# Broadcast row maxima put into query order by GpSimd once per group, with a new job order

## The reference, cut to what matters

```python
xn = layernorm(x)                      # x: 1 x 2048 x 256, eps 1e-5, no affine part
k, q, v = (einsum('ihd,bpd->biph', W, xn) for W in (W_K, W_Q, W_V))      # 16 heads of 128
scores = einsum('biph,biqh->biqp', k, q)
masked = scores * tril - 1e10 * (1 - tril)
attn = softmax(masked / sqrt(128), axis=-1)
s = einsum('df,bqf->bqd', W_O, concat_heads(attn @ v))
base = xn @ W_base.T + b_base
onehot = one_hot(argmax(softmax(xn @ router_W.T)), 8)                    # one of 8 experts of rank 16
g = silu(base + 2.0 * ((xn @ A) * onehot) @ Bw)
return x + s * g
```

## Time and profile before

| | |
|---|---|
| median of three runs | 1547.8 us |
| profiled execution, its own time | 1548.1 us |
| its span, first to last instruction | 1546.2 us |
| mean granted TensorE clock | 0.989 of full speed |
| score tiles, seeds of them by ScalarE | 640 |
| groups (head, g), each with its two DMAs | 64 |

### The profile page before, as it was taken

The page is one execution under the profiler, slowest core; times in us unless marked ns, Lnnn a source line. Parts: engine busy times, 40 slices in busy tenths (PEclk is TensorE's granted clock), DMA queues, the critical chain, the costliest instruction groups (busy, mean ns, idle before and its releaser), DMA issues.

```text
span 1546.2 us, 23204 instructions
## 1 busy us (share of the span) xinstructions
PE 1459.5 (94%) x7788; PEld 1193.2 (77%) x7788; DVE 1248.1 (81%) x2541; ACT 1274.0 (82%) x2196; POOL 793.4 (51%) x688
## 2 busy tenths in 40 slices
PE   5999999999999999999999999999999999999997
PEld 4877778777877878777787777877787777877765
DVE  6788877888788886888868887788878898788864
ACT  2788898889888898898988888888987988888962
POOL 2444655455465555456554555554645555544740
PEclk9899999999999999999999999999999999999998
DMA  2100010000100001000010001000010000100002
GB/s 75 49 8 14 15 25 25 15 15 8 29 21 15 15 7 42 15 14 13 10 42 15 7 15 28 22 15 14 8 35 21 15 7 13 40 8 15 15 28 82
DMA packets 30070, 33.75 MB, mean 22 GB/s; under 512 B 11008, under 2 KB 17664, under 8 KB 29952
## 3 DMA queue, kind: packets, MB, share of 16 engines
q1 hardware_dynamic: 29952, 32.26, 8.3%
HBM read 30.02 MB, written 2.23 MB: 21 GB/s over the span
## 4 chain that ended last, share of the span: by engine, by line
PE 51%; ACT 24%; DVE 13%; issue 9%; POOL 2%; DMA 0%; SPq 0%; ACTq 0%; POOLq 0%; DVEq 0%
PE ps L281 15%; PE ps L282 14%; PE ps L283 14%; ACT ps L478 7%; ACT probs L498 7%; ACT p_hi L499 6%; DVE p_lo L551 6%; PE ps L719 4%; DVE partmax L566 3%; POOL colsum L433 2%; PE ps L754 2%; ACT qT_hi L486 1%; DVE z_lo L588 1%; ACT z_hi L504 1%; PE ps L731 1%
## 5 line engine op out<-in xcount | busy, mean ns | idle before, releaser
L433 POOL TENSOR_TENSOR colsum<-colsum,probs 128x512 f32<-128x512 f32 (+3 forms) x512 | 610.2, 1192 | 388.3 <-ACT probs L498 373.6
L478 ACT ACTIVATE ps<-maxrow 128x512 f32<-128x512 f32 (+3 forms) x640 | 645.3, 1008 | 8.9 <-DMA maxrow<-max_dram 8.7
L551 DVE TENSOR_TENSOR p_lo<-probs,p_hi 128x512 fp32r<-128x512 f32 (+3 forms) x640 | 614.9, 968 | 42.4 <-ACT p_hi L499 41.4
L498 ACT ACTIVATE probs<-ps 128x512 f32<-128x512 f32 (+3 forms) x640 | 362.9, 567 | 141.4 <-PE ps L731 74.8
L499 ACT ACTIVATE p_hi<-ps 128x512 fp32r<-128x512 f32 (+3 forms) x640 | 365.3, 571 | 0.0
L566 DVE TENSOR_REDUCE partmax<-ps 128x1 f32<-128x512 f32 x384 | 256.9, 679 | 10.4 <-PE ps L719 9.5
L281 PE MATMUL ps<-qT_hi,kT_hi 128*128 128x512 f32 (+3 forms) x640 | 247.6, 387 | 12.7 <-ACT ps L478 9.6
L281 PE MATMUL ps<-p_hi,v_hi 128*128 128x512 f32 (+3 forms) x640 | 241.7, 378 | 13.2 <-DVE p_lo L551 12.2
L282 PE MATMUL ps<-qT_lo,kT_hi 128*128 128x512 f32 (+3 forms) x640 | 234.3, 366 | 0.0
L283 PE MATMUL ps<-qT_hi,kT_lo 128*128 128x512 f32 (+3 forms) x640 | 233.9, 366 | 0.0
L282 PE MATMUL ps<-p_lo,v_hi 128*128 128x512 f32 (+3 forms) x640 | 233.5, 365 | 0.0
(11 more groups left out here) (106 smaller groups left out, 2174.8 us busy)
## 6 DMA issues: line engine op xcount, KB each, us to landing
maxrow<-max_dram SPq DMA_DIRECT2D x64, 256.0 KB, 3.8
wraw<-wqk_dram SPq DMA_DIRECT2D x16, 256.0 KB, 3.8
acc<-x_dram SPq DMA_DIRECT2D x4, 512.0 KB, 7.2
wraw<-wv_dram SPq DMA_DIRECT2D x8, 256.0 KB, 4.7
wraw<-wo_dram SPq DMA_DIRECT2D x8, 256.0 KB, 2.9
probs<-x_dram SPq DMA_DIRECT2D x4, 512.0 KB, 4.5
out_dram<-acc SPq DMA_DIRECT2D x4, 512.0 KB, 3.0
max_dram<-rowmax SPq DMA_DIRECT2D x64, 2.0 KB, 1.4
```

What stands on the lines that cost most here:

```text
L433: nc.gpsimd.tensor_tensor(total[:, c0:], total[:, c0:], tile[:, c0:], ALU.add)\
L478: nc.scalar.activation(st[job.n % SCORE_BANKS].rearrange("p (t n) -> p t n", t=TB)[:, q:, :], maxrow[:, job.g, :].rearrange("p (n t) -> p ...
L498: nc.scalar.activation(probs[:, k, c0:], src, ACT.Exp, scale=SCALE).then_inc(probs_ready, 1)
L551: nc.vector.tensor_tensor(p_lo[:, k, c0:], probs[:, k, c0:], f32(p_hi[:, k, c0:]), ALU.subtract)\
```

## The change

GpSimd gets a new step, `order_maxima`: for each group it copies the broadcast row from a new buffer `spread` (two slots, used in turn) into `maxrow`, reading with a step of four elements and writing with step one, so that `maxrow` is in query order. ScalarE's seed reads `maxrow` with step one, waits at a group's first tile for GpSimd's `max_ordered` in place of the DMA, and writes the same columns as before. The step stands in GpSimd's queue ahead of the sum of tile min(slot of the last maximum + 6, first tile of the group - 2), and the first two groups' ahead of tile 0. It waits for the DMA and, from the second head on, for the seeds of the same g of the head before. SyncE's broadcast DMA waits for the copy two blocks back (`max_ordered`) in place of those seeds.

`SCHEDULE` holds the same 216 jobs in another order. The slots of the last maximum of each group (in the pair's 80 slots; first tile of the next pair's groups counted on from 80):

| group (head of the pair, g) | first score tile | last maximum before | after | copy ahead of tile |
|---|---|---|---|---|
| (0, 2) | 12 | 5 | 5 | 10 |
| (0, 3) | 24 | 18 | 17 | 22 |
| (1, 0) | 40 | 28 | 33 | 38 |
| (1, 1) | 44 | 37 | 37 | 42 |
| (1, 2) | 52 | 46 | 43 | 49 |
| (1, 3) | 64 | 58 | 57 | 62 |
| next (0, 0) | 80 | 73 | 71 | 77 |
| next (0, 1) | 84 | 79 | 79 | 82 |

The diff, with most of the written-out order cut:

```diff
--- before.py
+++ after.py
@@ -33,6 +33,7 @@
 PROBS = LAG + 1
 SCORE_BANKS = 3
 SEED_AHEAD = 2
+ORDER_LAG = 6
 AUX_BANKS = 3
 MASKED = -1.0e10
 SCALING = 2.0
@@ -101,16 +102,16 @@
 
 
 SCHEDULE = (
-    "V00 w Pq03 V01 w w z7 | | Pk02 | s7 Pk03 v V11 | o70 v M0222 | M0212 o71 v M0202 M0232 v | V21 S0 Z0 | v V10 "
...
 )
 AFTER_LAST = "w w w z7 s7 o70 o71"
 
@@ -186,6 +187,7 @@
         colsum = sb("colsum", [P, 2, BW])
         partmax = sb("partmax", [P, NB, TB, NB])
         rowmax = sb("rowmax", [P, NB, TB])
+        spread = sb("spread", [P, 2, BW])
         maxrow = sb("maxrow", [P, NB, BW])
         rinv = sb("rinv", [P, 2, TB])
         acc = sb("acc", [P, NT, D])
@@ -239,7 +241,8 @@
         aux_free = sem("aux_free")
         max_ready = sem("max_ready")
         max_out = sem("max_out")
-        max_spread = [sem(f"max_spread{g}") for g in range(NB)]
+        max_spread = [sem(f"max_spread{k}") for k in range(2)]
+        max_ordered = sem("max_ordered")
         bits_set = sem("bits_set")
         seeded = sem("seeded")
         scores_ready = sem("scores_ready")
@@ -267,6 +270,15 @@
             return NB + b if head % 2 and b < 2 else b
 
         scores = [job for job in plan if isinstance(job, Score)]
+        first_tile = {job.head * NB + job.g: job.n for job in scores if job.kt == 0}
+        max_blocks = [job.head * NB + job.g for job in plan if isinstance(job, RowMax) and job.last]
+
+        order_at, tile = [], 0
+        for job in plan:
+            if isinstance(job, Score):
+                tile = job.n + 1
+            elif isinstance(job, RowMax) and job.last:
+                order_at.append(tile and min(tile - 1 + ORDER_LAG, first_tile[job.head * NB + job.g] - SEED_AHEAD))
 
         def columns(t):
 
@@ -340,9 +352,10 @@
                     sp.wait_ge(max_ready, blocks)
                     sp.dma_start(row.rearrange("(p t) -> p t", t=TB), rowmax[:, job.g, :]).then_inc(max_out, 16)
                     sp.wait_ge(max_out, 16 * blocks)
-                    if job.head:
-                        sp.wait_ge(seeded, tiles_until((job.head - 1) * NB + job.g))
-                    sp.dma_start(maxrow[:, job.g, :], row.partition_broadcast(P)).then_inc(max_spread[job.g], 16)
+                    k = (blocks - 1) % 2
+                    if blocks > 2:
+                        sp.wait_ge(max_ordered, blocks - 2)
+                    sp.dma_start(spread[:, k, :], row.partition_broadcast(P)).then_inc(max_spread[k], 16)
                 if not isinstance(job, Score):
                     continue
                 i, at, last = job.n // TILES, job.n % TILES, job.n // TILES == PAIRS - 1
@@ -410,14 +423,27 @@
             split_weights(wraw[:, 0, :], flat(wqk_hi[:, 0]), flat(wqk_lo[:, 0]), wqk_in, 16, 1, wqk_ready)
             split_weights(wraw[:, 1, :], flat(wv_hi[:, :, :]), flat(wv_lo[:, :, :]), wv_in, 16, 2, wv_ready)
 
+            def order_maxima(block):
+
+                gi = max_blocks[block]
+                pool.wait_ge(max_spread[block % 2], 16 * (block // 2 + 1))
+                if gi >= NB:
+                    pool.wait_ge(seeded, tiles_until(gi - NB))
+                nc.gpsimd.tensor_copy(maxrow[:, gi % NB, :].rearrange("p (t n) -> p t n", t=TB),
+                                      spread[:, block % 2, :].rearrange("p (n t) -> p t n", t=TB))\
+                  .then_inc(max_ordered, 1)
+
             normed_jobs = sum(isinstance(job, Normed) for job in plan)
             pool.wait_ge(aux_full, normed_jobs)
             nc.gpsimd.memset(acc[:, :, :], 0.0).then_inc(acc_clear, 1)
-            his = 2
+            his, ordered = 2, 0
             for job in plan:
                 if not isinstance(job, Score):
                     continue
                 n, c0 = job.n, columns(job)
+                while ordered < len(max_blocks) and order_at[ordered] <= n:
+                    order_maxima(ordered)
+                    ordered += 1
                 gi = job.head * NB + job.g
                 total, tile = colsum[:, gi % 2, :], probs[:, n % PROBS, :]
                 pool.wait_ge(probs_ready, n + 1)
@@ -473,11 +499,10 @@
                 if job.n >= SCORE_BANKS:
                     act.wait_ge(hi_ready, job.n - SCORE_BANKS + 1)
                 if job.kt == 0:
-                    act.wait_ge(max_spread[job.g], 16 * (job.head + 1))
-                q = columns(job) // P
-                nc.scalar.activation(st[job.n % SCORE_BANKS].rearrange("p (t n) -> p t n", t=TB)[:, q:, :],
-                                     maxrow[:, job.g, :].rearrange("p (n t) -> p t n", t=TB)[:, q:, :],
-                                     ACT.Copy, scale=-1.0).then_inc(seeded, 1)
+                    act.wait_ge(max_ordered, max_blocks.index(job.head * NB + job.g) + 1)
+                c0 = columns(job)
+                nc.scalar.activation(st[job.n % SCORE_BANKS][:, c0:], maxrow[:, job.g, c0:], ACT.Copy, scale=-1.0)\
+                  .then_inc(seeded, 1)
 
             for job in plan:
                 if isinstance(job, (Normed, Project, ProjectV)):
```

## The result

The changed kernel takes 1452.07 us (median of 4 runs, 1448.1 to 1454.84) against 1547.76; the ratio is 0.9379 with a 95% interval of 0.9353 to 0.9405. That is 96 us, where 55 were forecast, and outside the range; it lies in the range of rival (1), 1440 to 1474 us.

What follows compares the result with a forecast made beforehand. A pipeline of three nearly full engines, TensorE first, waiting some 120 us of its 1460 us main part. Sum: 1548.1 - 37 - 12 - 5 + 5 + 3 - 9 = 1493 us; forecast 1475 to 1515, 8-in-10 range 1463 to 1528.

Steps and rivals of the forecast that it cites:

- rival (1): Everything TensorE waits for goes through ScalarE, and the order fills the rest: 1440 to 1474 us; chance 0.15.
- the tally of 1340 us: TensorE's counted work in the main part of 1460 us, leaving some 120 us of waiting.
- What it is worth: Step pricing the shorter seed by TensorE's waits: -37 us on seeds, -12 on `p_lo`, -5 on VectorE's other work.
- the 49 us: TensorE's waits put down to VectorE's reductions and evacuations, taken as VectorE's own queue; only 5 us expected to go.
- half of the 25 for `p_lo`: TensorE's 25 us of waits on `p_lo`: p_hi sits behind shorter seeds, so half goes, -12 us.
- The term for the copies: GpSimd's copies add 20 us to VectorE's 1248 by blocking; a quarter reaches TensorE, +5 us (+2 to +15).
- The 0.25 us of blocking per us of GpSimd's work: Rate from VectorE's `p_lo` beside GpSimd: 202 us lost per 793 of GpSimd, applied to 77 us of copies.
- The order: New job order: same jobs, may use the room ScalarE has gained, -9 us, bounds -25 and +15.
- the added wait: Copy between the broadcast's landing and a group's first seed: path 5.6 to 6.9 us, +3 in all (0 to +30).
- rival (4): Same time: late copies in GpSimd's queue delay sums and hold probs, 51 us against 54 gained: 1545 to 1551; chance 0.04.
- Rival (2): VectorE becomes the bound; seed waits turn into waits for `p_lo` or reductions: 1535 us, 1516 to 1545; chance 0.14.
- Rival (3): Slower: ScalarE's seed stays at 1155 ns because the PSUM write sets it: 1566 us; chance 0.05.

Runs made afterwards that it cites:

- e9: Kernel before, old order, with step-one seeds straight from the broadcast row; no copy, no putting into query order: 1448.25 us, ratio 0.9351.
- e12: e9 with each seed cut into two pieces of 256 columns: 1447.87 us, ratio 0.9341.
- e13: e9 with each seed cut into four pieces of 128 columns: 1481.28 us, ratio 0.9557.
- e11: Kernel before, long seeds and old order, with GpSimd's running sums cut to their last 128 columns: 1510.18 us, ratio 0.9742.
- e14: e9 with GpSimd's sums also cut to their last 128 columns, as in e11: 1441.41 us, ratio 0.9312.
- e15: e9 with a 64-column VectorE memset ahead of each `p_lo`: 1449.97 us, ratio 0.9364.
- e8: Kernel before in the new order, with step-one seeds straight from the broadcast row; no copy, no putting into query order: 1454.21 us, ratio 0.9384.
- e1: Kernel after, with step-one seeds and GpSimd's copies, in the old order: 1482.24 us, ratio 0.9564.
- e2: Kernel before, strided seeds and no copies, with the new `SCHEDULE`: 1531.22 us, ratio 0.9878.
- e3: Kernel after with the strided seed: GpSimd copies strided in and out, ScalarE reads with step four: 1537.63 us, ratio 0.9927.
- v2: Kernel after in the old order, each group's first seed reading the broadcast row itself with step four: 1457.87 us, ratio 0.9405.

## Why the prediction was wrong

**Right.** The seed (620 ns forecast, 615 measured), the copy (1.2, 1.201), TensorE's pace and the tally of 1340 us, the last group's loop (1.45 to 1.55 forecast, 1.48), and that waits on the seed nearly vanish. The copy costs nothing that can be told in the new order where I had 8 us. ScalarE's busy time came to 1032, not 990: its records overlap less where it has gaps (the records' sum fell by 343 us, their overlap by 101).

**The step that failed** is this one of "What it is worth": the 49 us "are VectorE's own queue; only its waits for ScalarE's copies shorten: -5", and with it only half of the 25 for `p_lo`. I read the engine named last in a wait as the one that owns it. e9 refutes that: with VectorE's program and the order untouched, these waits went with the seed. From before to e9 the weight loads' waits fell by 45 us on the seed, where I took 37, by 16 on `p_lo`, where I took 12, and by 31 on the reductions of the earlier trace rows alone, where I took 5 for everything of that kind. I took -54 for the seed; it is -100, and in the kernel after 26 us of waiting are left in the main part, of 120.

What carries it is shown in part. VectorE's queue stands behind ScalarE's at every evacuation and every `p_lo`, so a ScalarE that answers late shows as a VectorE that ends late. The pieces of e12 and e13 show that the size follows the length of the seeds, with a threshold between 1.57 and 1.75 us a tile in ScalarE's loop. e11 shows that a lighter VectorE alone, 159 us off it where the seed took 54, gives 38 of the 100 us; so at least 62 need ScalarE's own relief, if more relief of VectorE never costs time. e14 shows that the two reliefs are for the most part the same microseconds (38 alone, 7 with short seeds). How much of the remaining 38 went through VectorE stays open: e15, meant to settle it, put no load on VectorE.

**VectorE's load** went down by 73 us, not up by 20. The term for the copies was not far off: from e8 to the kernel after they add 12 us, from e9 to e1 16, from e2 to e3 7. What the prediction had at nothing is what the rest of the change does to `p_lo`: the short seed takes 54 us off VectorE (before to e9), the new order another 31 (e9 to e8). The 0.25 us of blocking per us of GpSimd's work belongs to the slow loop of the earlier trace rows, in which `p_lo` arrives 0.4 us into an add. Counted over the two timelines, 319 of the 448 full `p_lo` start while GpSimd is at work in the kernel before (1.33 us each), and 278 in the kernel after (1.12 us each); the others take 0.68 in both. GpSimd's 512-column add went the other way, from 1412 to 1504 ns.

**The order** was mis-sized: -9 taken. It is -17 with the old seed (e2), -30 with seeds and copies (e1 to after) and -3 or so with no copy (e8 and e9, from the first `p_lo` to the last). Its gain here is chiefly the room it makes for the copy: in the old order copies cost 34 us (1482.24 against 1448.25), in the new one none (1452.07 against 1454.21). In the old order it is the added wait that costs, for which I took +3 with bounds of 0 to +30: first seeds wait for the copy (74.8 us in e1), and v2, in which they don't, wins 24 of the 34 back. It is not rival (4), whose price was the sums: the exponentials wait 0.5 us in all for them in e1. So the change is -100 for the seed, +34 for copies in the old order, -30 for the new one.

**The others.** Rival (1), given 0.15, has the right time and half the mechanism: what TensorE waited for hung on ScalarE, but the order did not fill the rest, it only made room for the copy. My reason against it, VectorE's 86%, took blocked time as fixed work. Rival (2) rested on the same misreading. Rival (3) is excluded by the 615 ns.

## What to carry to other kernels

When several engines in one ring are over 80% busy, don't share out the bottleneck's waits by the engine that ended them. Take the loop of the engine to be relieved, tile by tile; where it is well above the bottleneck's pace (here 1.96 us against 1.38), give a good chance to the case that nearly all of the waiting is its own. Below a threshold, here between 1.57 and 1.75, relieving it further brings nothing. Time in which one engine is held up by another is part of its busy time, but its rate doesn't carry over to another rhythm. And price an order by what it gives to a new wait, here 5 to 7 slots for a copy in place of 4 for most of the tight groups. Before a run with an added load is read, look whether the load took any time: e15's did not.

## What the runs showed of the hardware

- ScalarE's Copy from SBUF to PSUM takes 615 ns at 512 columns with step one and 1155 with a source step of 16 bytes. The Trainium skill (SBUF — State Buffer, "Door 1: The DMA port swizzle") has reads pay where each falls into a new line of 16 bytes and names a stride of 4 fp32 as still free; here a stride of exactly 4 costs 540 ns, which fits the first of these and not the second.
- GpSimd's copy reading with that step takes 1201 ns for 512 elements in the kernel after, beside the 1.24 us estimated from the Trainium skill (GPSIMD Engine Reference, "Performance pitfalls for Q7 kernels"); in the old order (e1) the same copy takes 1359.
- A VectorE memset of 64 columns, 0.11 us on record, cost no time ahead of a 512-column subtraction, which started 0.03 us behind it (e15).
- TensorE's granted clock in the last stage was 0.76 in the profiled runs of the kernel after and of e8, that is partly at the 1.2 GHz level, and 0.91 in those of the kernel before and of e9. From the last `p_lo` on this stage takes 55.2 us at 0.76 and 48.2 at 0.91. TensorE had been busy for over 99% of the main part in after, e8 and e9 alike, so its busy share there doesn't tell which one comes; the cause is open. Over the four runs of the kernel after the mean clocks 0.985, 0.986, 0.990 and 0.991 go with 1454.8, 1454.2, 1448.1 and 1450.0 us, so its median lies between two levels some 6 us apart.
